# Final two heads of the last attention group taken token tile by token tile, GpSimd normalising, and gathered expert rows added one at a time

## The reference

```python
def reference(x, ctx_2048, ...):
    x = x + jnp.tanh(g_xattn[0]) * _L0_xattn_ref(_layernorm(x), ctx_2048, Wq, bq, Wkv, bkv, Wp, bp)
    x = x + jnp.tanh(g_ffn[0]) * _L0_ffn_ref(_layernorm(x), Wg, W1, W3, W2, Ws1, Ws3, Ws2)
    return x

# _L0_xattn_ref: 16 heads of 32; q, k in int8 steps per row, v in int8 steps per channel over all keys
    attn = jax.nn.softmax(jnp.einsum('bhqd,bhkd->bhqk', q, k), axis=-1)
    attn = _fq_unsigned(attn, axis=-1)            # 255 steps of the row's maximum
    out = jnp.einsum('bhqk,bhkd->bhqd', attn, v)
    return out.transpose(...).reshape(B, N, C) @ Wp + bp

# _L0_ffn_ref: 16 routed experts (best 2 of 4 groups, 4 experts per token) and 2 shared ones
    h = silu(einsum('td,eid->eti', xt, W1)) * einsum('td,eid->eti', xt, W3)
    y = einsum('etd,te->td', einsum('eti,edi->etd', h, W2), combine)
    z = silu(xt @ Ws1.T) * (xt @ Ws3.T) @ Ws2.T
    return (y + z).reshape(B, S, D)
```

## Time and profile before

| | us |
|---|---|
| median of 3 runs (1069.75 to 1071.2) | 1069.77 |
| the profiled execution's own time | 1069.22 |
| its span, first to last instruction | 1067.7 |
| last exponentials end, in the span | 599.3 |
| first shared-expert product, in the span | 656.2 |
| last gathered tile finished, in the span | 1063.1 |
| busy shares PE, DVE, ACT, POOL | 93%, 60%, 47%, 40% |

### The profile page before, as it was taken

One profiled execution on the slowest core, in us unless ns is written; L12 is line 12 of the kernel. 1 busy time (PEld: TensorE's weight loads), 2 busy tenths in 40 slices (PEclk: granted clock), 3 DMA queues, 4 the chain that ended last, 5 costly groups with the idle time before them and its releaser, 6 DMA issues.

```text
span 1067.7 us, 16598 instructions
## 1 busy us (share of the span) xinstructions
PE 988.1 (93%) x5718; PEld 500.9 (47%) x5719; DVE 644.1 (60%) x1140; ACT 499.1 (47%) x1072; POOL 431.7 (40%) x293
## 2 busy tenths in 40 slices
PE   5999999879999999999999699999999999999993
PEld 2334444324444444444444356555665665565551
DVE  4895766599999999999999545821111111111156
ACT  2022222259999999999999532111221122122110
POOL 1043333217777777777677500171111111111065
PEclk9999999989999999999999788999999999999996
DMA  9954655688888888888786444154445655653155
GB/s 321 226 200 178 208 192 202 195 152 146 139 139 130 141 140 143 142 138 133 133 136 111 68 168 168 39 199 141 167 176 183 230 191 188 236 181 114 49 166 152
DMA packets 268272, 172.45 MB, mean 162 GB/s; under 512 B 239344, under 2 KB 239344, under 8 KB 265904
## 3 DMA queue, kind: packets, MB, share of 16 engines
q1 hardware_dynamic: 258512, 140.14, 54.2%
q0 software_dynamic: 9696, 31.47, 8.7%
HBM read 68.67 MB, written 44.63 MB: 106 GB/s over the span
## 4 chain that ended last, share of the span: by engine, by line
PE 56%; DVE 16%; POOL 11%; ACT 8%; issue 6%; DMA 3%; SPq 0%; POOLq 0%; DVEq 0%; ACTq 0%
PE ps L692 17%; PE ps L712 10%; POOL arena_a L1349 8%; PE ps L577 8%; ACT arena_a L866 7%; PE ps L560 6%; PE ps L537 5%; DVE span_max L1052 4%; PE ps L619 3%; POOL expert_in L1358 2%; PE ps L662 2%; PE ps L722 1%; DVE v_q L1273 1%; PE ps L703 1%; DVE proj_i L1011 1%
## 5 line engine op out<-in xcount | busy, mean ns | idle before, releaser
L1052 DVE TENSOR_REDUCE span_max<-ps 128x1 f32<-128x481 f32 (+2 forms) x400 | 351.4, 904 | 17.5 <-PE ps L577 8.4
L866 ACT ACTIVATE arena_a<-ps,exp_bias,q_step 128x962 uint8<-128x962 f32 (+1 forms) x288 | 329.7, 1156 | 20.7 <-DVE exp_bias L1072 11.2
L1349 POOL CAST arena_a<-arena_a 128x3072 bf16<-128x3072 uint8 x100 | 273.7, 2747 | 129.3 <-DMA arena_a<-arena_a 119.0
L577 PE MATMUL ps<-arena_a,q_t 128*128 128x481 bf16 (+1 forms) x864 | 224.4, 372 | 18.6 <-DVE span_max L1052 7.0
L692 PE MATMUL ps<-arena_a,xt 128*128 x544 | 172.2, 459 | 1.7 <-issue 1.7
L1211 DVE TENSOR_TENSOR proj_d<-ps,proj_f 128x352 f32<-128x352 f32 x48 | 25.1, 524 | 205.5 <-ACT proj_f L901 205.4
L712 PE MATMUL ps<-arena_a,proj_r 128*128 (+3 forms) x288 | 134.1, 602 | 0.7 <-ACT proj_r L907 0.7
L907 ACT COPY proj_r<-ps 128x128 f32<-128x128 f32 x144 | 28.4, 270 | 227.1 <-PE ps L703 227.1
L577 PEld LDWEIGHTS ps<-arena_a,q_t 128*128 128x128 bf16 x864 | 61.5, 97 | 148.9 <-ACT arena_a L866 73.0
L692 PEld LDWEIGHTS ps<-arena_a,xt 128*128 128x128 f32 x544 | 100.4, 190 | 61.2 <-issue 17.9
L619 PEld LDWEIGHTS ps<-v_q,arena_a 128*128 128x128 bf16 x2400 | 77.0, 97 | 31.2 <-POOL arena_a L1349 12.8
(11 more groups left out here) (166 smaller groups left out, 909.6 us busy)
## 6 DMA issues: line engine op xcount, KB each, us to landing
arena_a<-in_w_up SPq DMA_DIRECT2D x18, 1408.0 KB, 6.4
arena_a<-in_w_down SPq DMA_DIRECT2D x18, 768.0 KB, 8.4
key_parts<-parts SPq DMA_DIRECT2D x23, 512.0 KB, 2.6
expert_in<-xt SPq DMA_DIRECT2D x42, 256.0 KB, 3.0
xt<-expert_in POOLq DMA_DIRECT2D x36, 256.0 KB, 3.0
expert_out<-xt POOLq DMA_DIRECT2D x34, 256.0 KB, 2.3
arena_a<-in_ctx_t SPq DMA_DIRECT2D x3, 1536.0 KB, 13.6
expert_out<-xt SPq DMA_DIRECT2D x17, 256.0 KB, 3.1
```

Of the source, the lines that this page charges most:

```text
L577: last = mm(ps[:, bank + b, 0:w], q_t[:, head, t * P:(t + 1) * P], k_t[head % NK][:, a:a + w], start=True, stop=True)
L866: nc.scalar.activation(halves[:, :, a:a + w], ps[:, bank:bank + 2, 0:w], ACT.Exp, bias=exp_bias[:, n % 2:n % 2 + 1], scale=step_of, accum_ ...
L1052: v.tensor_reduce(span_max[:, n % 2, j:j + 1], ps[:, bank:bank + len(blocks), 0:w], AX.XY, ALU.max).then_inc(s_max, 1)
L1349: p.tensor_copy(p_t[n % NPT].rearrange("p c q -> p (c q)").rearrange("p (j i) -> p j i", j=2), pt_u8[n % NT8].rearrange("p (i j) -> p j i" ...
```

## The change

Three edits.

1. **Order of the last group.** In the last group (tiles 75 to 99) heads 12 and 13 stay head by head (75 to 86). Heads 14 and 15 go token tile by token tile: (14, 0), (15, 0), (14, 1), (15, 1), the tail tile, (14, 2), (15, 2) and so on to (15, 5). So token tiles are complete at n = 88, 90, 93, 95, 97, 99 (`COMPLETE`), the tail at 91. DVE inverts the sums of each tile three tiles after it is complete, inside the loop of maxima, and the last after it; POOL bounds the inverses from below and normalises behind one of its casts (behind cast 91, 93, 94, 96, 98, 98, 99). PE's transposes, projections and last value products are woven together, the normed rows' transposes in banks 5 and 6 of PSUM.
2. **`v_step` is put on the weights.** POOL multiplies the four parts of `wp_sb` by it behind casts 12 to 15, and ACT copies a transposed tile in one piece instead of four.
3. **Gathered rows one by one.** `ADDED` = 0, 4, 10, 16, 28 rows are added by shared tile 9, 10, 11, 12, 13, before the shared product of the same token tile is there; a token tile is finished once both are in.

```diff
-    COMBINED = [[], [], [0, 1], [2, 3], [4], [5, 6]]
+    ADDED = [0, 4, 10, 16, 4 * T]
...
+        for t in range(T - 1):
+            LAST_PLACES += [(NG - 1, H - 2, t), (NG - 1, H - 1, t)]
+            if t == 1:
+                LAST_PLACES.append((NG - 1, None, T - 1))
...
# PE
+            for n in range(NTILE + 1):
+                attention_step(n)
+            pe.wait_ge(s_max, NM * NTILE)
+            turn_attention(0)
+            turn_attention(1)
+            weigh_values(NTILE - 3)
+            turn_attention(2)
+            pe.wait_ge(s_wps, DC)
+            project_out(0)
+            weigh_values(NTILE - 2)
+            turn_attention(3)
+            turn_attention(4)
+            pe.wait_ge(s_exp, NE * NTILE)
+            project_out(1)
+            weigh_values(NTILE - 1)
+            project_out(2)
+            turn_attention(5)
+            project_out(3)
+            turn_attention(6)
+            turn_normed(0)
+            project_out(4)
+            turn_normed(1)
+            project_out(5)
+            turn_normed(2)
+            route(0)
+            project_out(6)
+            for t in range(3, T):
+                turn_normed(t)
+                route(t - 2)
+            route(T - 2)
+            route(T - 1).then_inc(s_lg, 1)
...
# DVE
-            dve.wait_ge(s_exp, NE * NTILE)
-            for inv, sums in ((inv_sum[:, :, 0:T - 1], exp_sums[:, :, 0:T - 1, :]), (tail_inv[:, :], tail_sums[:, :, :])):
-                link(v.tensor_reduce(inv, sums, AX.X, ALU.add))
-                link(v.reciprocal(inv, inv))
-                link(v.tensor_scalar(inv, inv, 1e-8, None, ALU.max))
...
+                for t in range(T - 1):
+                    if n == COMPLETE[t] + INV_LAG:
+                        invert_tile(t)
+                if n == LAST_TAIL + INV_LAG:
+                    invert_tails()
...
+                while added < ADDED[k]:
+                    add_gathered(added)
+                    added += 1
+
+                    if added == (finished + 1) * TOPK and finished <= u - 1 - T:
+                        finish(finished, pairs * 2 + u)
+                        finished += 1
+            dve.wait_ge(s_comb, T * TOPK)
             keep_shared(SU - 1, pairs * 2 + SU - 1)
...
# POOL
+            def normalise(i, done, t):
+                pool.wait_ge(s_inv, i + 1)
+                pool.wait_ge(s_ao, done + 1)
+                inv = tail_inv[:, :] if t is None else inv_sum[:, :, t]
+                p.tensor_scalar(inv, inv, 1e-8, None, ALU.max).then_inc(s_low, 1)
+                pool.wait_ge(s_low, i + 1)
...
+                    p.tensor_tensor(a, a, spread(inv, [P, H, HD]), ALU.mult).then_inc(s_attn, 1)
...
+                for i, (done, t) in enumerate(INV_ORDER):
+                    if n == min(done + 3, max(done, NTILE - 2)):
+                        normalise(i, done, t)
+                if 12 <= n < 12 + DC:
+                    p.tensor_scalar(wp_sb[:, n - 12, :], wp_sb[:, n - 12, :], v_step[:, n - 12:n - 11], None,
+                                    ALU.mult).then_inc(s_wps, 1)
```

More of the change, by code:

```diff
@@ L629, in _, with attention_step @@
             for_exp(0, 1)
-            for n in range(NTILE + 4):
+            def attention_step(n):
                 if n >= 2:
@@ L645, in _, with turn_attention @@
                 for_max(n + 1, 1)
-            for t in range(T):
+            def turn_attention(t):
                 if t < T - 1:
@@ L676, in _, with project_out, turn_normed @@
-            last.then_inc(s_lg, 1)
+            def project_out(t):
+                pe.wait_ge(s_ot, t + 1)
+                if t >= 2:
+                    pe.wait_ge(s_x1, t - 1)
+                for k in range(DC):
+                    last = mm(ps[:, 2 + t % 2, :], attn_t[:, k, t * P:(t + 1) * P], wp_sb[:, k, :],
+                              start=(k == 0), stop=(k == DC - 1))
+                last.then_inc(s_out, 1)
+            def turn_normed(t):
+                pe.wait_ge(s_xn, T + t + 1)
+                transpose_tile(xn, t, s_tr, s_xt, T, 5)
@@ new lines, in route @@
+            def route(r):
+                pe.wait_ge(s_xt, T + r + 1)
+                for k in range(DC):
+                    last = mm(ps[:, 4, r * E:(r + 1) * E], x2_t[:, k, r * P:(r + 1) * P], wg_sb[:, k, :],
+                              start=(k == 0), stop=(k == DC - 1))
+                return last
+            for n in range(NTILE + 1):
[4 more added lines that the diff above has]
+            weigh_values(NTILE - 3)
@@ L1044, in _, with invert, invert_tile, invert_tails @@
             link(v.tensor_scalar(neg_tail_step[:, :], tail_step[:, :], -1.0, None, ALU.mult))
+            def invert(inv, sums):
+                link(v.tensor_reduce(inv, sums, AX.X, ALU.add))
+                v.reciprocal(inv, inv).then_inc(s_inv, 1)
+            def invert_tile(t):
+                dve.wait_ge(s_exp, NE * (COMPLETE[t] + 1))
+                invert(inv_sum[:, :, t], exp_sums[:, :, t, :])
+            def invert_tails():
+                dve.wait_ge(s_exp, NE * (LAST_TAIL + 1))
+                invert(tail_inv[:, :], tail_sums[:, :, :])
             def maximum(n, j):
@@ L1276, in combine, with finish @@
+            def finish(t, kept):
+                rows = P if t < T - 1 else TAIL
                 dve.wait_ge(s_comb, (t + 1) * TOPK)
+                dve.wait_ge(s_ya, kept)
                 v.scalar_tensor_tensor(y_sb[0:rows, t, :], y_sb[0:rows, t, :], gates[0:rows, 1:2],
                                        x_sb[0:rows, t, :], ALU.mult, ALU.add).then_inc(s_store, 1)
-            for u in range(PRE, SU):
+            added, finished = 0, 0
+            for k in range(POST):
+                u = PRE + k
@@ L1291, in _ @@
+            dve.wait_ge(s_comb, T * TOPK)
             keep_shared(SU - 1, pairs * 2 + SU - 1)
-            dve.wait_ge(s_ya, pairs * 2 + SU)
-            for t in COMBINED[POST]:
-                combine(t)
+            for t in range(finished, T):
+                finish(t, pairs * 2 + SU)
         @block.gpsimd
```

125 lines of the change are left out of this document (63 added, 62 removed).

## The result

The changed kernel takes **1052.99 us** (median of four runs, 1051.98 to 1058.07), against 1069.76 us; the ratio is 0.9846 with a 95% interval from 0.9822 to 0.9870. It is faster, 16.8 us by the medians. The forecast was 1057.7 us with a range down to 1054.5: the gain was under-estimated by 4.7 us, and the time lies outside the range.

A forecast was written before the change was run, and what follows sets the result against it. It took DVE to set attention's pace and PE's idle time after attention as the main hole. Terms -10.9 + 0.3 - 1.5 = -12.1 us gave 1057.1 from the profiled 1069.22, 1057.7 as median; range 1054.5 to 1063.

The forecast's parts named there:

- the scaled weights: Scaling `wp_sb` on POOL behind casts 12 to 15: 0.3 us on the path, bounds 0 and 0.9.
- the small waits and the clock of the transition: Between attention and first shared product: 1.5 us added for small waits, 2.0 for a fall of PE's clock.
- the pace of the gathers: At the end: 28 gathers at 1.109 us with 0.30 between, 39.2 us in all.
- What bounds the kernel, and the order's effect: After attention, nearly 20 us hold little PE work; the new order brings the first shared product 10.9 us earlier.
- order without effect: After attention: PE's in-order list waits for POOL, so projections start no earlier than POOL ends; 1063 us; chance 0.06, shared.
- Part 1: Attention loop: inversions on DVE cost 2.3 us, all on the path, the tail in mid-stream 1.1; exponentials 3.4 later.
- Part 2: Casts and normalisations on POOL near attention's end: 34.8 us of work fits into 36.5, 1.7 to spare.
- GpSimd becomes the bound: Attention's end: normalisations over 1.8 us each, so the nine casts no longer fit; 1062.5 us, chance 0.12.
- Part 3: PE after attention: first projection at about 604.5, first shared product at 645.4 instead of 656.3 us.
- the clock stays low: After attention: PE at half speed until 640 would lose 18 us; 1073.7 us, slower than before, chance 0.03.
- Part 4: Program end: the ring no longer stops POOL's gathers; last finish 0.2 to 2.7 us earlier, 1.5 taken.
- more than forecast: Whole kernel: no fall of the clock, small waits gone, quick landing at the end; 1054.5 us, chance 0.08.

The follow-up runs named there:

- the repeat: The changed kernel itself run once more, unaltered, on the same chip in the rounds of later experiments: 1055.20 us.
- a2_end_only: The kernel before with only the third edit (gathered rows added one by one), attention and transition unchanged: 1067.83 us, ratio 0.9977.
- the other mends: The changed kernel with the weight scalings spread out, the tail tile last and the last shared product added before the tail's gathered rows: 1054.26 us.

## Why the prediction was right, and where not

The hole in PE closed as told, but the sum fell short by 4.3 us in the profiled execution. The terms that failed are what attention pays (2.0 too much), the scaled weights (1.05 too little), the small waits and the clock of the transition (1.4 too much) and the pace of the gathers with what follows them (2.1 too much).

- **What bounds the kernel, and the order's effect: right.** The hole closes in the way told. First projection 1.4 us after the last exponentials (forecast 1.8), 40.3 us from there to the first shared product (forecast 40.9); PE ends on its own work, with one wait of 1.2 us for a normalisation. The rival *order without effect* is out.
- **Part 1, what attention pays: size wrong, 3.4 forecast, 1.4 measured.** The step that failed is "all on the path (bound: 0, if DVE had hidden slack, which the gapless period speaks against)". DVE waits for PE about 0.2 us in each period, just where the inversions stand; five cost about 0.6 us in all and not 2.3, and doubling them showed that the second of a pair is paid in full. The tail in mid-stream cost about 0.9 (taken 1.1, bounds 0.73 to 1.5), mostly by its value product.
- **Part 2, GpSimd: right in its upshot.** A token tile's normalisation took 1.4 us (0.27 and 1.08, with what lies between; forecast 1.55), twice 1.8 to 1.9. Cast 99 ended at 612.4 (forecast 612.7). But "covered" was not quite so: PE waited 1.2 us for tile 4. The prediction looked at cast 99 and the last normalisation only; by its own figures the two normalisations ahead of cast 99 end at 610.0, while PE comes to the transpose of tile 4 at about 609.4. The rival *GpSimd becomes the bound* is out.
- **The scaled weights: size wrong, +0.3 forecast, +1.35 measured,** outside the bounds of 0 and 0.9. I had summed what each operation took beyond the spare time but took their duration from other forms: 1.56 us is above both rows that I used as bounds.
- **Part 3, the clock: right in kind.** I counted 2.0 us for a fall between 600 and 620; the profiled execution had none, the repeat had one. What I did not see is that both kernels have a second fall at the router's logits, whose length changes from run to run (7, 10 or 14 us in the traces), and that the kernel before was read in an execution where it was short: 56.9 us from exponentials to shared product, 59.8 in a2_end_only with the same code. The rival *the clock stays low* is out.
- **Part 4, the end: direction right, 1.5 forecast, 2.8 measured, and 0.6 to 0.8 behind it.** The ring's stop went as told. The step that failed is the pace, "28 gathers at 1.109 us": this mean contains POOL's hindrance by DVE's blocks of adds. Spread adds hinder less (1.062 us), so the last gather starts 36.75 us after the first where 38.1 was forecast. POOL's issue is not all that is late next, either: up to the last finish, the chain ends with 6.3 us of DVE's work without a stop, and the issue of the last four gathers is not in it. `gate(13)` was late and PE waited 1.5 us, without effect, as told.

Their sum, term by term: -2.0 (attention), +1.05 (weights), -0.9 and -0.5 (transition), -1.3 and -0.8 (end), +0.2 elsewhere, together -4.3, from -12.1 to -16.4. The case "more than forecast" was the one that came; of its reasons the missing fall of the clock held in this execution, the largest one, attention's price, was not among them. The range was too narrow below for two reasons. That case was added up wrongly: by the prediction's own figures its three reasons are 2.0, 1.5 and up to 1.2 us, which gives 1053.0 and not 1054.5, and the lower bound of the inversions was not in it at all. And nothing in the range stood for the spread of the runs: three had shown 1.5 us, while most kernels here show 4 to 7. So it is partly chance on which side of 1054.5 a median falls: the repeat's 1055.20 lies inside. The mis-sized terms do not depend on that, since they are read from stretches.

What makes the start, up to tile 11, differ by up to 4 us between executions (265.4 to 269.5) is also the clock. Eight of the fourteen traces have a fall at about 78 us, and in them the first bias comes at 222.4 to 223.7 us, in the other six at 220.7 to 221.4. And all have one from about 221 us on: where it lasts 7 us, it takes 43.9 us from the first bias to that of tile 11, where it lasts 10 us 44.4 to 44.8, where it lasts 14 us 45.6 to 45.9. Still open is what decides whether and for how long the clock falls in one execution.

## What to carry to other kernels

Where an engine's rows look gapless, look for the wait in the groups by form before calling it the pace, and test by doubling: the first addition may be free and the second not. Work put on GpSimd is priced against what VectorE does at that moment, and the other way round; moving it between the two may change nothing. And where a stretch of small products and waits stands in TensorE's list, put full-width work that is ready into it: here one product moved some 8 us forward gained 4.9 us and gave 1.7 back, more than the 2.3 of the other mends together.

## What the hardware showed

A two-input product on VectorE, 0.69 us alone, took 3.12 and 3.17 us behind a GpSimd cast and ended half a microsecond after it. GpSimd's scaling of 128x512 by a scalar for each partition took 1.56 us, longer than its product of two tensors of that size (1.08). The granted clock fell in the same place of the same kernel in one execution and not in another, and a fall avoided in one place came up at a later idle time, at 711 us.
